# A two-block transformer kernel in float32: the last batch's maxima moved into the stage before, a vector turned on TensorE, GpSimd additions in halves

## What is computed

```python
h = layernorm(x) * (1 + ca) + sa;  x = x + ga * attention0(h)   # causal, 16 heads of 64
h = layernorm(x) * (1 + cb) + sb;  x = x + gb * mod_ffn(h)      # a router picks 127 of 1024 tokens
h = layernorm(x) * (1 + ca) + sa;  x = x + ga * attention1(h)   # full, 16 heads of 8, 3d rope, biases
h = layernorm(x) * (1 + cb) + sb;  x = x + gb * moe(h)          # 8 experts, the best 2 by softmax
```

## Time and profile before

| | |
|---|---|
| median of 3 runs | 2725.14 us (2724.52 to 2730.5) |
| profiled execution | 2733.0 us, span 2731.2 us |
| mean granted TensorE clock | 0.918 |
| busy PE, PEld | 2183.8 (80%), 896.9 (33%) |
| busy DVE, ACT, POOL | 1627.4 (60%), 1276.4 (47%), 804.2 (29%) |

### The profile page before, as it was taken

The page is one execution under the profiler, slowest core; times in us unless marked ns, Lnnn a source line. Parts: engine busy times, 40 slices in busy tenths (PEclk is TensorE's granted clock), DMA queues, the critical chain, the costliest instruction groups (busy, mean ns, idle before and its releaser), DMA issues.

```text
span 2731.2 us, 39653 instructions
## 1 busy us (share of the span) xinstructions
PE 2183.8 (80%) x14753; PEld 896.9 (33%) x14757; DVE 1627.4 (60%) x2829; ACT 1276.4 (47%) x2289; POOL 804.2 (29%) x618
## 2 busy tenths in 40 slices
PE   3989998899777887889868778888877677667876
PEld 2434443444321133444312123344432222121112
DVE  3454446556678556555676745655576776487732
ACT  1433333343358743343347763233336466537873
POOL 0665563443500033443411103443343000001203
PEclk9999998999899998989989998898998898869999
DMA  3000001001110010000210000000021100110000
GB/s 79 15 23 15 20 23 35 23 27 35 35 42 14 1 30 12 15 19 27 66 40 20 12 4 27 19 15 27 12 65 38 47 1 16 59 34 3 5 3 8
DMA packets 81199, 69.14 MB, mean 25 GB/s; under 512 B 46672, under 2 KB 62800, under 8 KB 80496
## 3 DMA queue, kind: packets, MB, share of 16 engines
q1 hardware_dynamic: 81008, 66.60, 9.0%
HBM read 57.58 MB, written 8.98 MB: 24 GB/s over the span
## 4 chain that ended last, share of the span: by engine, by line
PE 61%; DVE 22%; ACT 9%; issue 6%; SPq 2%; DMA 1%; POOL 0%; ACTq 0%; POOLq 0%; DVEq 0%
PE banks L875 59%; DVE pmax L2342 5%; ACT ring L1765 3%; DVE part_max L1943 2%; ACT p_sum L1765 1%; ACT room L1572 1%; SPq L666 1%; DVE ntmp L1892 1%; PE banks L1014 1%; DVE ntmp L1847 1%; DVE pick L2083 1%; DVE rstd L1894 1%; DVE h L1911 1%; DVE room L2092 1%; DVE stats L1899 1%
## 5 line engine op out<-in xcount | busy, mean ns | idle before, releaser
L816 POOL TENSOR_TENSOR p_sum<-p_sum,ring 128x1024 f32<-128x1024 f32 (+3 forms) x320 | 548.9, 1715 | 810.5 <-PE banks L875 453.0
L2342 DVE TENSOR_REDUCE pmax<-banks 128x2 f32<-128x1024 f32 x512 | 610.5, 1222 | 187.9 <-PE banks L875 184.6
L1943 DVE TENSOR_REDUCE part_max<-banks 128x2 f32<-128x1024 f32 (+3 forms) x384 | 365.8, 958 | 336.7 <-PE banks L875 334.2
L875 PE MATMUL banks<-ring,v 128*9 128x512 f32 (+4 forms) x2816 | 565.5, 581 | 0.0
L875 PE MATMUL banks<-qT,kT 64*128 64x512 f32 (+4 forms) x2048 | 468.3, 521 | 100.1 <-DVE pmax L2342 52.4
L1765 ACT ACTIVATE ring<-banks 128x512 f32<-128x512 f32 x768 | 416.3, 596 | 144.7 <-PE banks L875 141.5
L1524 ACT ACTIVATE ring<-banks 128x1024 f32<-128x1024 f32 (+3 forms) x320 | 245.7, 768 | 473.9 <-PE banks L875 468.6
L875 PE MATMUL banks<-oT 64*128 64x512 bf16 x1024 | 185.2, 397 | 91.6 <-ACT ring L1765 41.7
L875 PEld LDWEIGHTS banks<-qT,kT 64*128 64x128 f32 (+1 forms) x2048 | 147.7, 169 | 325.0 <-issue 101.5
L875 PE MATMUL banks<-p_sum,v 128*9 128x512 f32 (+1 forms) x768 | 220.4, 644 | 31.9 <-DVE oT L1964 26.3
L847 POOL TENSOR_TENSOR room<-room 128x512 f32<-128x512 f32 x32 | 40.6, 1270 | 691.5 <-ACT room L1572 691.5
(11 more groups left out here) (270 smaller groups left out, 2624.7 us busy)
## 6 DMA issues: line engine op xcount, KB each, us to landing
inv_bc<-softmax_inverses SPq DMA_DIRECT2D x64, 256.0 KB, 4.0
w_qk<-in_L_attn_w_qkv SPq DMA_DIRECT2D x64, 64.0 KB, 2.1
low<-in_L_ffn_attention_mask SPq DMA_DIRECT2D x4, 1024.0 KB, 6.1
stage<-rope_constants SPq DMA_DIRECT2D x4, 1024.0 KB, 4.8
x_b<-in_L_attn_x SPq DMA_DIRECT2D x4, 512.0 KB, 4.6
w_v<-in_L_attn_w_qkv SPq DMA_DIRECT2D x32, 64.0 KB, 2.1
stage<-in_L_ffn_w SPq DMA_DIRECT2D x8, 256.0 KB, 6.2
out<-x_b SPq DMA_DIRECT2D x16, 128.0 KB, 1.8
```

What stands on the lines that cost most here:

```text
L816: pool.tensor_tensor(sv, sv, ring0[SLOT[m]][:, :, 0:HALF - lo], ALU.add).then_inc(sem("added"), 1)
L875: return pe.matmul(dst, lhsT, rhs, start=start, stop=stop)
L1943: dve.reduce_max(part_max[:, :, t, c], banks[MAX_PAIR[m]][:, :, 0:w], AX).then_inc(sem("row_max"), 1)
L2342: dve.reduce_max(pmax1[:, :, g, t, c], banks[(0, 3)[USE1[b]["max", m] % 2]][:, :, :], AX).then_inc(sem("row_max1"), 1)
```

## The change

1. ~wcol becomes a banked side step wcol: PE turns the row with 8 transposes of 1 x 128 into a column in PSUM, and DVE copies it twice. The copy of the constant "row" moves to the setup.
2. `add_up` issues two instructions, one for each half (128 x up to 512), with a wait between them.
3. The RMS norms call `rsqrt_column`, in which all three instructions of a Newton step are TENSOR_SCALAR with columns as scalars; layer norms keep `rsqrt`.
4. DVE reads mod0 and mod1 from PSUM itself; ACT's copies go; the gate rule has three instructions in place of five.
5. Batch 3 gets other rooms for its stacks (group 0 in the two free oT tiles, groups 1 to 3 in the rooms that groups 0 to 2 of batch 2 leave). Group g > 0 waits for batch 2's scores of groups below g alone. SP issues the experts' weights and the stacks at the end of `late_chain(B - 2)`, that is right behind ~split.
6. Batch 3's steps -24 to -2 are done behind steps 110 to 126 of batch 2 (`LAST_AT`; one or two each). Batch 3's own loop begins at -1.
7. To make room, MOD_ATTN and PREP of batch 3 are spread over steps 29 to 104 (~split at 103) in place of 29 to 127; v1_0 and v1_1 go to steps -1 and 0 of batch 3, mod1 to the last expert to steps 1 to 90.

```diff
+LAST_AT = {110 + n: range(-LEAD + 23 * n // 17, -LEAD + 23 * (n + 1) // 17) for n in range(17)}
...
     if b == B - 1:
-        return spread(steps, 1 - LEAD, 90)
-    cut, first, last = (len(MOE), 29, STEPS1 - 1) if b == B - 2 else (len(MOE), 97, 113)
+        return {-1: steps[:1], 0: steps[1:2], **spread(steps[2:], 1, 90)}
+    cut, first, last = (len(MOE), 29, 104) if b == B - 2 else (len(MOE), 97, 113)
...
-            n = NP * (b + 2)
-            rooms = [(kT[0], qT[0]), (kT[1], qT[1]), (oT[n % OSLOTS], oT[(n + 1) % OSLOTS]), (oT[(n + 2) % OSLOTS], oT[(n + 3) % OSLOTS])]
+            n = NP * (min(b, B - 2) + 2)
+            early, late = (oT[n % OSLOTS], oT[(n + 1) % OSLOTS]), (oT[(n + 2) % OSLOTS], oT[(n + 3) % OSLOTS])
+            rooms = [(kT[0], qT[0]), (kT[1], qT[1]), early, late]
+            if b == B - 1:
+                rooms = [(oT[(n + 4) % OSLOTS], oT[(n + 5) % OSLOTS])] + rooms[:3]
...
-                if b:
+                if b == B - 1:
+                    if g:
+                        sp.wait_ge(sem("st1_mm"), NI1 * (b - 1) + 2 * UI * g)
+                    else:
+                        sp.wait_ge(sem("out_mm"), 2 * b)
+                elif b:
                     sp.wait_ge(sem("st1_mm"), NI1 * b)
...
                     yield from prep_side(B - 1)
+                    load_experts(B)
+                    for g in range(NG):
+                        stack_group(B - 1, g)
...
-                    pool.tensor_tensor(sv, sv, ring0[SLOT[m]][:, :, 0:HALF - lo], ALU.add).then_inc(sem("added"), 1)
+                    pool.tensor_tensor(sv[:, 0, :], sv[:, 0, :], ring0[SLOT[m]][:, 0, 0:HALF - lo], ALU.add).then_inc(sem("added0"), 1)
+                    pool.wait_ge(sem("added0"), NA * n + ADDED[m])
+                    pool.tensor_tensor(sv[:, 1, :], sv[:, 1, :], ring0[SLOT[m]][:, 1, 0:HALF - lo], ALU.add).then_inc(sem("added"), 1)
...
+                side_free(("wcol", b))
+                read_out(pe, ("w1", b))
+                for t in range(T):
+                    last = pe.transpose(side[:, t:t + 1], w_row[0:1, t * P:(t + 1) * P], eye[0:1, 0:1])
+                last.then_inc(sem("side_mm"), 1)
+                yield "wcol"
...
                         step1(a - 1, k, steps)
+                        for last in LAST_AT.get(k, ()) if a + 1 == B else ():
+                            step1(B - 1, last)
...
-            for k in range(-LEAD, STEPS1):
+            for k in range(-1, STEPS1):
                 step1(B - 1, k, steps)
...
+            def rsqrt_column(dst, src, bits, t_):
+
+                link(dve.tensor_scalar(bits, src.bitcast(I32), 1, None, ALU.logical_shift_right))
+                link(dve.tensor_scalar(bits, bits, -1.0, RSQRT_MAGIC, ALU.mult, ALU.add))
+                cur = bits.bitcast(F32)
+                for _ in range(3):
+                    link(dve.tensor_scalar(t_, cur, cur, -0.5, ALU.mult, ALU.mult))
+                    link(dve.tensor_scalar(t_, t_, src, 1.5, ALU.mult, ALU.add))
+                    link(dve.tensor_scalar(dst, t_, cur, None, ALU.mult))
+                    cur = dst
...
-                link(dve.scalar_tensor_tensor(ga, g, -1.0, g, ALU.mult, ALU.max))
-                link(dve.tensor_scalar(ga, ga, 0.25, None, ALU.max))
-                link(dve.tensor_scalar(g, g, 0.0, 2.0, ALU.is_ge, ALU.mult))
-                link(dve.tensor_scalar(g, g, -1.0, None, ALU.add))
-                link(tt(g, g, ga, ALU.mult))
+                link(dve.tensor_scalar(dst, g, 0.0, 0.5, ALU.is_ge, ALU.subtract))
+                link(dve.scalar_tensor_tensor(ga, dst, 4.0, g, ALU.mult, ALU.mult))
+                return dve.scalar_tensor_tensor(dst, ga, 0.5, dst, ALU.max, ALU.mult)
...
-                for t in range(T):
-                    dve.scalar_tensor_tensor(ties[:, t, :], w_row[:, t * P:(t + 1) * P], 1.0, eye, ALU.mult, ALU.mult, accum_out=w_col[:, t:t + 1]).then_inc(sem("w_col"), 1)
-                dve.wait_ge(sem("w_col"), T * (b + 1))
-                link(dve.tensor_copy(extra[:, :, 0], w_col[:, :]))
+                filled(dve, ("wcol", b))
+                link(dve.tensor_copy(extra[:, :, 0], side[:, 0:T]))
+                dve.tensor_copy(w_col[:, :], side[:, 0:T]).then_inc(sem("side_out"), 1)
+                read_out(dve, ("wcol", b))
```

More of the change, by code:

```diff
@@ L108, in exp_item1, with step_uses1 @@
     return u, r // GH, r % GH
+def step_uses1(b, k):
+    order = []
+    if k + LEAD < STEPS1:
+        order.append(("max", k + LEAD, b))
+    if k + LEAD in ROWS_AT:
+        order.append(("row", ROWS_AT[k + LEAD], b))
+    if k in CTX_AT:
+        order.append(("ctx", CTX_AT[k], b))
+    if k in OUT_AT and b + 1 < B:
+        order.append(("out", OUT_AT[k], b))
+    for step in LATE_STEPS[b].get(k, ()) if b in LATE_STEPS else ():
+        if step[0][0] != "~":
+            order.append(("side", step, b))
+    return order
 def uses_of_pairs1(b):
@@ L114, in uses_of_pairs1 @@
     for k in range(-LEAD, STEPS1):
-        if k + LEAD < STEPS1:
-            order.append(("max", k + LEAD))
-        if k + LEAD in ROWS_AT:
-            order.append(("row", ROWS_AT[k + LEAD]))
-        if k in CTX_AT:
-            order.append(("ctx", CTX_AT[k]))
-        if k in OUT_AT and b + 1 < B:
-            order.append(("out", OUT_AT[k]))
-        for step in LATE_STEPS[b].get(k, ()) if b in LATE_STEPS else ():
-            if step[0][0] != "~":
-                order.append(("side", step))
+        order += step_uses1(b, k)
+        for last in LAST_AT.get(k, ()) if b == B - 2 else ():
+            order += step_uses1(B - 1, last)
+    if b == B - 2:
+        for k in range(-1, STEPS1):
+            order += step_uses1(B - 1, k)
     return order
-MOD0 = ["mod0", "~gates0"]
+MOD0 = ["mod0"]
 ADD1 = ["mod1", "ctxT0", "ctxT1", "wo1_0", "wo1_1"]
@@ L759, in _ @@
                     load_weights(NP * (a + 1) + 1)
-            load_experts(B)
-            for g in range(NG):
-                stack_group(B - 1, g)
             straight(late_chain(B - 1))
@@ L1024, in mod0_side @@
                 yield "mod0"
-                yield "~gates0"
             def add1_side(m):
@@ L1588, in mod_side @@
                     yield f"w{c}"
-                for s in MOD_ATTN[MOD_ATTN.index("~wcol"):MOD_ATTN.index("pickT0")]:
+                for s in MOD_ATTN[MOD_ATTN.index("wcol"):MOD_ATTN.index("pickT0")]:
                     yield s
```

75 lines of the change are left out of this document (36 added, 39 removed).

## The result

Measured after the change: 2620.07 us median (2618.45 to 2626.31), before, on the same chip, 2727.06 us (2724.52 to 2730.5). The ratio is 0.9611, 95% interval 0.959 to 0.9632: 106 us faster. The direction was right and the size was off by a factor of two. (The profiled execution of after took 2621.42 us, with a span of 2619.6.)

A forecast was written before the change was run, and what follows sets the result against it. PE was taken to set the pace where fed, with DVE, held by POOL's lock, and the batch 2 to 3 gap starving it. Terms -16 - 21 + 2 + 0 - 13 = -48, plus 3 for clock: -51 from 2725.1, 2674 us; range 2640 to 2708.

The forecast's parts named there:

- the 3 us for PE's clock: Whole kernel: 3 us faster allowed because a stretch with fewer holes should not be granted a clock of 0.85.
- A, router weights: Turning of router weights: 28.6 us leave DVE, 20 reach the end, less four new PE steps; net -16, from -28 to -2.
- the factor of 0.7: Share of removed DVE time at router weights and roots taken to reach the end, between 0.5 and 1 for the router weights.
- B, roots: Inverse roots on one column: POOL does not block the new form; 0.7 of 30.4 us gone, -21, from -30 to -8.
- C, halves: POOL additions in halves: +5 at the keys' cast, -3 from shorter DVE waits; +2 us, from -15 to +15.
- The sign named for it: For the halved additions: the largest DVE wait would be about 1.3 us in place of 2.5.
- D, gates: Gates read from PSUM: as many DVE instructions or fewer, ACT's 8 copies off the chain; 0 us, from -4 to +2.
- E, batch 3: Change from batch 2 to 3: gap -49.5, side steps +12, moved steps +23, steps 104 to 127 +1.4; -13, from -38 to +7.
- Rival 3: More than forecast: every lock removed reaches the end, batch 3's move gives -25; 80 us faster, 2645 us; chance 0.16.
- Rivals 1 and 5: 1: DVE waits move on, 2692 us, 0.16. 5: that, no transition gain and halves at their bad end, 2725 us, 0.03.
- Rival 4: First attention: POOL sets the pace if the wait between halves costs 0.5 us, deciding from 0.35; 2754 us, chance 0.06.
- Rival 2: Batch 3 transition gives nothing: PE waits 14 us at step 110, side steps cost 3 us each; +7, 2694 us; chance 0.14.

## Why the prediction was wrong in size, and where it was right

In the three stages before the second attentions the sum had 38 us and 82 came. Two of its steps failed there: the 3 us for PE's clock, which are 19 to 26, and the gates at nothing, which over the whole run are 23 with the new places that they give to other steps. At the change of batches it had 13 and 25 came, since two costs set against the gap were too high.

**A, router weights** (-16). The gain is 29 us alone and 11 on top of the others. The 28.6 us that go from DVE were right: over the whole run DVE is busy 1627.4 us before and 1598.5 with this part. The step that failed is the factor of 0.7 as a fixed share of what reaches the end: with the long waits still there the part is worth 29 us, as much as all of its 28.6, and with the other parts in place 11, less than the 16 forecast.

**B, roots** (-21). 37 us alone, 17 on top. That POOL does not block the column form was right, in every one of 72 instances, 48 of which ran while POOL was at work; a pointer scalar costs 0.06 us more, so that the sign given for it (nothing over 0.2 us) was missed by 0.014. The rule that was cited (the Trainium skill, SBUF — State Buffer, section SBUF: two separate sides), by which a DVE instruction with two SBUF tensors meets POOL's lock, agrees with what was held. That columns read as scalars do not count as such tensors is what this run shows.

**C, halves** (+2). On top of the others the halves cost 2 us by the medians of the ratios (0.9611 to 0.9604), and within the intervals nothing. The forecast had 2 us as well, but the noise is too large for that to confirm it. The handover of 0.08 was exact, and so was POOL's own growth. The first contexts of batch 0's pairs 0 and 2 start at 79.2 and 147.0 in the kernel before and at 79.1 and 147.4 after, 33.9 and 34.15 us a pair: the quarter of a microsecond that a pair is longer was costed as 0.32, for the keys' cast. With whole additions the same two stand at 77.9 and 145.7, 33.9 us a pair again; that it is the cast which makes the difference is not shown further.

```profile
L1964 DVE COPY oT<-banks x5: 681/681/681, 79.2 to 147.0; 128x512 f32<-128x512 f32 x5
```

```profile
L1999 DVE COPY oT<-banks x5: 678/681/681, 79.1 to 147.4; 128x512 f32<-128x512 f32 x5
```

What failed is the gain's size where the waits are long: alone the halves give 37 us. The sum had -3, since each half of a linked sequence was to catch one; they did not, and still less did each half hold DVE once more (the +5 of the prediction). The sign named for it failed too: the longest held product took 2.20 us in the changed kernel (L2135), not 1.3.

**D, gates** (0, from -4 to +2). Undone, they cost 23 us. The step that failed is "as many DVE instructions or fewer", priced by count alone: 8 us are the new places of all later steps, which the prediction did not name at all, and 15 the work itself. Why the work is worth 15 is open; the runs do not part the copies by ACT from the six instructions on SBUF. In the profiles 8 us of it lie before the first exponential of batch 0 (751.1 us without the new gates, 743.1 with them at the old places).

**The clock** (-3). This is the term furthest off. Over the three stages PE is busy 645.9 + 346.7 + 345.6 = 1338.2 us in the kernel before and 637.7 + 337.0 + 337.1 = 1311.8 with all but batch 3: 26 us, with 84.7 us less time. The other 58.3 are PE's idle time, for 66.2 us less of DVE. By the profile of the run with batch 3 alone, which has the same code in these stages as before (PE busy 1333.8), and that of the changed kernel (1314.7) the clock's part is 19, so it is some 19 to 26 us where the sum had 3. The idle part is 56 to 58 where A to D had 35, and in it are the places and the gates' work that the sum had at nothing. The windows at the 6.7 us wait show how the clock's part comes about. That a shorter hole alone lifts the clock is read from the windows of each run, and was not tried by filling a hole with work.

**E, batch 3** (-13). 25 us, alone and on top. By its own parts:

| part | forecast | stages and rows |
|---|---|---|
| gap | -49.5 | -49.7 (53.5 to 3.8) |
| the lead's six side steps | +12 | +1.6 (batch 3's loop 230.9 to 232.5) |
| steps 28 to 103 | +23 | +13.7 (190.9 to 204.6) |
| steps 104 to 127 | +1.4 | +6.2 (46.4 to 52.6) |
| sum | -13 | -28 (the run alone: -25) |

Two steps failed: the 12 us, since six side steps that cost 2 us each in the lead, where no exponential ran, are hidden nearly whole in batch 3's loop; and the 23 us, where the ten moved steps cost 13.7 with all else that stands there. The run with this part alone has the same four rows (53.5 to 3.8, 232.6, 206.1, 52.6), -27 in sum. The wait at step 110 is 3.2 us and not 7; that stretch is longer all the same, at a granted 0.81 where it was 0.93.

**The rivals.** Rival 3 named the side on which the result lies, with each lock wait reaching the end, and still fell 25 us short, for the same two terms, clock and places. Rivals 1 and 5 had waits that move on to other instructions. Some do (L2135 went from 349 to 551 ns, 6.5 us in all), but DVE as a whole was busy 66.2 us less in the three stages. Rival 4 needed a handover of 0.35 us, and it is 0.08. Rival 2 needed all of 14 us at step 110, and it is 3.2; its own terms (-49.5 + 12 + 33 + 8.4) add to +4 and not to the +7 that it was given, which changes nothing else.

## To carry to other kernels

Where one engine feeds another in order, ask of each wait how long a hole it makes in the fed engine whose clock falls when it stands, and not only how long it is: over the three stages here 1 us less of DVE went with 0.9 us less idle PE and 0.3 to 0.4 us of clock. That is a mean and no price: for the idle part it was 0.5 in the first stage, and 2.7 where places alone were moved. Where side work is laid out by an even spread, a step more or less moves many others, and here six trials of places alone moved the time by 0 to 32 us; rebuild the layout and read which items each step now stands behind before pricing anything at zero. Parts that shorten the same waits do not add (here 37, 29 and 37 us alone, but 17, 11 and nothing when taken out): test each both alone and taken out.

## What was not expected of the hardware

- A DVE instruction on one column with its scalars read by pointer takes 214 ns, against 153 with immediate ones, and was never held by POOL in 72 instances, 48 of them beside a POOL instruction (the row gives shortest, median and longest of 24), though it reads all its operands from SBUF.
- A cast of 128 x 8 from float to bf16 with one input (L2392) is held when it meets POOL (12 of 64, 374 to 853 ns) where a free one takes 174, while the maximum on as many columns beside it (L2391) never takes over 172, in 12 meetings as well.
- POOL held a linked DVE sequence only as long as its own work lasted, so repeating the sequence at once added little more than its free price: 0.35 us for each of 32 products whose first 32 took 0.77 with their waits.
- After a hole of 6.7 us PE ran its next 8 us at a granted 0.56, though busy for 7.4 of them.

```profile
L1930 DVE TENSOR_SCALAR ntmp<-ntmp,nvar x24: 211/214/216, 479.3 to 2183.6; 128x1 f32<-128x1 f32 x24
```

```profile
L2391 DVE TENSOR_REDUCE nmax<-pmax x64: 154/166/172, 725.6 to 2508.0; 128x8 f32<-128x16 f32 x64
```

```profile
L2392 DVE CAST nmax_hl<-nmax x64: 173/174/853, 725.8 to 2508.2; 128x8 bf16<-128x8 f32 x64
```
